# Attention on one Trainium2 core: the low parts of the probabilities on VectorE, made in halves of 256 columns

## The chip, the cores and the metric

One NeuronCore of a Trainium2 chip. The metric is the time of one launch of the whole program on the device, in microseconds (us). Engines are named as in the profile: PE is TensorE (PEld its weight loads), DVE is VectorE, ACT is ScalarE, POOL is GpSimd, SP is the queue that issues most DMAs.

## The reference

The input x has shape (2, 8, 256, 512): batch, channel, row, column. It is normalised by groups, goes through attention, and the result is added to x; then it is normalised again and goes through a sphere convolution, which is added too. Only the attention matters for this change:

```
q = _rope(split_heads(_conv(_mcl(x, Wq, bq), q_conv_w, q_conv_b, 3)))
k = _rope(split_heads(_conv(_mcl(x, Wk, bk), k_conv_w, k_conv_b, 3)))
v = split_heads(_conv(_mcl(x, Wv, bv), v_conv_w, v_conv_b, 3))
qk = jnp.einsum('bceqd,bcekd->bceqk', q, k) / math.sqrt(h)
a = jax.nn.softmax(qk, axis=-1)
o = jnp.einsum('bceqk,bcekd->bceqd', a, v)
return _conv(_mcl(o, Wo, bo), o_conv_w, o_conv_b, 0)
```

For each of the 2 x 8 pairs of batch entry and channel there are 8 heads with 512 queries, 512 keys and 32 features a head.

## The kernel before, in words

The program has three stages one behind the other, each with a block of its own: `front` (normalisation, projections, convolution, rotation), `attend` (attention), `blend` (mixing, second normalisation, sphere convolution). The change lies in `attend`, which in the profile runs from about 375 to about 890 us.

`attend` handles 16 units, one for each pair of batch entry and channel. A unit has 32 steps: 8 heads times 4 tiles of 128. Several things happen for each step, shifted against one another:

- **Row scores** (`row_scores`, L1197): PE multiplies 128 queries by all 512 keys into one of three PSUM banks called `a_row`. DVE takes the maximum of each row (`row_max`, L1265), and then the bank is free. The maxima of a unit are split in two (L1269), turned by PE (L1206, also into an `a_row` bank), copied by ACT (L1294) and put into the query tile as two more rows, so that the next pass subtracts them.
- **Column scores** (`col_scores`, L1217): PE makes the scores again, transposed, into one of three banks `a_col`; ACT takes the exponential into `a_prob`, float32 128x512 (L1306).
- **Low parts**: the matmuls that follow work in bfloat16. The upper 16 bits of each probability serve as its high part `ph`, read with a stride in the float32 tile. The low part is `prob` minus `ph`, written as bfloat16 into `a_pl`. Of the 32 steps of a unit, 26 are done by POOL (L1349) and six by DVE (L1276), those of `LOWS_ON_DVE = (1, 5, 9, 23, 26, 30)`. Both engines read two tensors from SBUF and write one. Below, such an instruction is called a low.
- **Sets**: after each four steps PE sums the weights (L1231) and mixes the values (L1240), 20 matmuls of 32 output rows each, four side by side. After four sets ACT makes the logarithm and the inverse of the weights (L1311, L1318) and DVE multiplies the mix by it (`divide`, L1284).
- **Tails**: PE multiplies the divided result by the output weights (L1254) into a further `a_row` bank, which is held for ten steps; ACT copies it out (L1324).

Each engine's instructions are written out in order by `pipeline(ops)`: every operation has a slot number, and an engine emits its operations slot by slot. Row work of step t of unit n has slot 32n + t; the low of that step has slot 32n + 43 + t on both engines, which is why lows of one unit lie between row maxima of the next two. The set g of a unit has slot 32n + 54 + 4g on PE, so 8 slots lie between the last low of a set and the set.

`row_places()` fixes at build time which of the three `a_row` banks a row score, a turn of the maxima or a tail gets: the one used longest ago that is not held. In the steady state the row score of place r in a unit (r = slot modulo 32) therefore waits for the row maximum of place r - 3 for r = 6 to 22. From r = 23 on to r = 4 of the next unit the tail, and after it the turn, takes one of the banks in the rotation, and the row score of place r waits for the row maximum of place r - 2. At r = 5 it waits for the bank of the turn, which the copy L1294 on ACT frees. I count places r in what follows: the lows of DVE stand behind the row maxima of places 2, 5, 9, 12, 16 and 20, the two divides behind those of places 3 and 19, the tail begins behind the set at place 22.

The waits of the row bank and of the set on PE:

```
s_row = bank_free(pe, ROW_PLACE[step])      # waits for max_done, among others
...
pe.wait_ge(lo_pool, pool_lows(n, g))
pe.wait_ge(lo_dve, dve_lows(n, g))
```

Of the kernel before, what the change touches and what calls it, by code (L numbers as in the profile page):

```python
# [20 lines left out]
ALU = mybir.AluOpType  # L21
# [3 lines left out]
B, C, F, W = 2, 8, 256, 512  # L25
# [908 lines left out]
def attend(nc, T, QK, V, Z, mixing, spaces, q0, k0, qk0_in, negmax0, ahead_in):  # L934
# [9 lines left out]
    with ExitStack() as ctx:  # L944
# [3 lines left out]
        STEPS = HEADS * QT  # L948
        UNITS = B * C
# [20 lines left out]
        prob = [sb(f"a_prob{s}", [P, QUAD, W]) for s in range(RING)]  # L970
        ph = [prob[s][:].bitcast(BF16).rearrange("p h (w t) -> p h w t", t=2)[:, :, :, 1] for s in range(RING)]
        pl = [sb(f"a_pl{s}", [P, QUAD, W], BF16) for s in range(RING)]
# [27 lines left out]
        lo_dve = sem("a_lo_dve")  # L1000
# [20 lines left out]
        def low_on_pool(t):  # L1021

            return t not in LOWS_ON_DVE

        def dve_lows(n, g):

            return len(LOWS_ON_DVE) * n + sum(t < QUAD * (g + 1) for t in LOWS_ON_DVE)

        def pool_lows(n, g):

            return STEPS * n + QUAD * (g + 1) - dve_lows(n, g)


        SPLIT = STEPS
        TURN = SPLIT + 3
        EXP = TURN + 7
        MIX = EXP + 3 * QUAD
        KEEP = MIX + QUAD * (QT - 1) + 1
        TAIL = KEEP + QUAD * QT + 3
        PARTS = 2  # L1040
        PART = W // PARTS
        assert TURN + STEPS < TAIL and TAIL + 2 * (QT + 1) < TURN + 2 * STEPS

        def pipeline(ops):

            at = [[] for _ in range(UNITS * STEPS + TAIL)]
            for t, f in ops:
                at[t].append(f)
            for slot in at:
                for f in slot:  # L1050
                    f()

        def steps(first, emit):
            return [(STEPS * n + first + t, lambda n=n, t=t: emit(n, t)) for n in range(UNITS) for t in range(STEPS)]

        def rows(emit):
            return [(STEPS * n + t, lambda n=n, t=t: emit(n, t)) for n in range(UNITS) for t in range(STEPS) if STEPS * n + t >= EARLY]

        def lows(first, emit, on_pool):
            return [(STEPS * n + first + t, lambda n=n, t=t: emit(n, t)) for n in range(UNITS) for t in range(STEPS) if low_on_pool(t) == on_pool]  # L1060

        def sets(first, emit):
            return [(STEPS * n + first + QUAD * g, lambda n=n, g=g: emit(n, g)) for n in range(UNITS) for g in range(SETS)]

        def quads(first, emit):
            return [(STEPS * n + first + QUAD * QT * m, lambda n=n, m=m: emit(n, m)) for n in range(UNITS) for m in range(SETS // QT)]

        def units(first, emit):
            return [(STEPS * n + first, lambda n=n: emit(n)) for n in range(UNITS)]

        def tails(first, emit):
            return [(STEPS * n + first + (QT + 1) * j, lambda n=n, j=j: emit(n, j)) for n in range(UNITS) for j in range(FH)]

        def tail_parts(first, emit):
            return [(STEPS * n + first + (QT + 1) * j + QT // PARTS * part, lambda n=n, j=j, part=part: emit(n, j, part))
                    for n in range(UNITS) for j in range(FH) for part in range(PARTS)]

        def row_places():
# [10 lines left out]

            for at in range(UNITS * STEPS + TAIL):  # L1090
                n, t = divmod(at - TURN, STEPS)
# [3 lines left out]
                if EARLY <= at < UNITS * STEPS:  # L1095
                    rows[at] = take(at)
                    maxima[rows[at][0]] = at + 1 - EARLY
                n, t = divmod(at - TAIL, STEPS)
                if t == 0 and 0 <= n < UNITS:
# [80 lines left out]
        def _(pe):  # L1180
# [39 lines left out]
            def mix_set(n, g):  # L1220
                kt, quad = g % QT, SETS // QT * n + g // QT
                p = (SETS * n + g) % RING
                pe.wait_ge(lo_pool, pool_lows(n, g))
                pe.wait_ge(lo_dve, dve_lows(n, g))
                if n == g == 0:
                    pe.wait_ge(ones_set, 1)
                if kt == 0 and quad:
                    pe.wait_ge(logged, quad)
                for part in (ph, pl):
                    for r in range(QUAD):  # L1230
                        nc.tensor.matmul(weight[r * DH:(r + 1) * DH, :], ones[:], part[p][:, r, :],  # L1231
                                         start=kt == 0 and part is ph, stop=kt == QT - 1 and part is pl)
                if g == 0:
                    pe.wait_ge(v_in[n % VALUES], 16 * (n // VALUES + 1))
                if kt == 0 and quad:
                    pe.wait_ge(divided, quad)
                for j, (vv, part) in enumerate(((vh, ph), (vl, ph), (vh, pl))):
                    for r in range(QUAD):
                        h = g // QT * QUAD + r
                        last = nc.tensor.matmul(mix[r * DH:(r + 1) * DH, :], vv[n % VALUES][:, kt, h * DH:(h + 1) * DH], part[p][:, r, :],  # L1240
                                                start=kt == j == 0, stop=kt == QT - 1 and j == 2)
                last.then_inc(mixed, 1)

            def tail(n, j, part):
# [8 lines left out]
                for f in range(FH):  # L1253
                    last = nc.tensor.matmul(out[n][:, at], wo[n % CHANNELS][:, f, j * P:(j + 1) * P], oT[n % 2][:, f, at], start=f == 0, stop=f == FH - 1)  # L1254
                if part == PARTS - 1:
                    last.then_inc(out_full, 1)

            pipeline(units(TURN, turn_max) + steps(EXP, col_scores) + rows(row_scores) + sets(MIX, mix_set) + tail_parts(TAIL, tail))

        @block.vector  # L1260
        def _(ve):
            def row_max(n, t):
                step = STEPS * n + t
                ve.wait_ge(row_full, step + 1 - EARLY)
                nc.vector.reduce_max(negmax[n % PAIR][:, 0, t:t + 1], row[ROW_PLACE[step][0]][:], AX.X, negate=True).then_inc(max_done, 1)  # L1265

            def split_max(n):
                ve.wait_ge(max_done, STEPS * (n + 1) - EARLY)
                nc.vector.tensor_tensor(negmax[n % PAIR][:, 1, :].rearrange("p (h t) -> p h t", t=QT), negmax[n % PAIR][:, 0, :].rearrange("p (h t) -> p h t", t=QT),  # L1269
                                        maxhigh[n % PAIR][:, 0:HEADS, :], ALU.subtract).then_inc(max_split, 1)  # L1270

            def low_part(n, t):
                step = STEPS * n + t
                p, r = step // QUAD % RING, t % QUAD
                ve.wait_ge(exp_done, step + 1)
                nc.vector.tensor_tensor(pl[p][:, r, :], prob[p][:, r, :], ph[p][:, r, :], ALU.subtract).then_inc(lo_dve, 1)  # L1276

            def divide(n, m):
                quad = SETS // QT * n + m
                if m == 0 and n >= 2:  # L1280
                    ve.wait_ge(out_full, FH * (n - 1))
                ve.wait_ge(mixed, QT * (quad + 1))
                ve.wait_ge(inverted, quad + 1)
                nc.vector.tensor_tensor(oT[n % 2][:, m, :], mix[:], inverse[quad % 2][:], ALU.mult).then_inc(divided, 1)  # L1284

            pipeline(rows(row_max) + units(SPLIT, split_max) + lows(EXP + 1, low_part, False) + quads(KEEP, divide))

        @block.scalar
        def _(act):
# [36 lines left out]
            def store_z(n, j):  # L1326
# [3 lines left out]
            pipeline(quads(KEEP, log_weight) + units(TURN + 1, keep_max) + units(TURN + 2, load_max) + steps(EXP, exp) + quads(KEEP, invert)  # L1330
                     + tails(TAIL + QT, keep_out) + tails(TAIL + QT + 1, store_z))
            for j in range(FH):
                act.wait_ge(z_stored[j], 16 * UNITS)

        @block.gpsimd
        def _(pool):
            nc.gpsimd.memset(ones[:], 1.0).then_inc(ones_set, 1)
            pool.wait_ge(ones_set, 1)
            nc.gpsimd.memset(wmix[:], 0.0).then_inc(wzero, 1)
            pool.wait_ge(wzero, 1)  # L1340
            nc.gpsimd.memset(w_taps[:, 1], 0.0).then_inc(wzero, 1)
            pool.wait_ge(const_in, 16)
            nc.gpsimd.tensor_copy(ident16[:], ident[:]).then_inc(ident16_set, 1)

            def low_part(n, t):
                step = STEPS * n + t
                p, r = step // QUAD % RING, t % QUAD
                pool.wait_ge(exp_done, step + 1)
                nc.gpsimd.tensor_tensor(pl[p][:, r, :], prob[p][:, r, :], ph[p][:, r, :], ALU.subtract).then_inc(lo_pool, 1)  # L1349

            pipeline(lows(EXP + 1, low_part, True))

# [559 lines left out]
```

## Time and profile before

| | |
|---|---|
| median of 3 runs | 1157.39 us (1154.14 to 1162.59) |
| the profiled execution, its own time | 1156.79 us |
| span of the profiled execution | 1154.9 us |
| PE busy | 1051.2 us (91%) |
| DVE busy | 827.7 us (72%) |
| ACT busy | 682.9 us (59%) |
| POOL busy | 745.9 us (65%) |

The span runs from the first to the last instruction of the profile; the time of the execution is 1.9 us longer. Busy times are averages over three stages with different limits. What a change inside `attend` is worth has to be read from the stretch between about 400 and 880 us, in which one unit follows another in the same pattern.

### The profile page before, as it was taken

The numbers are of one execution on the slowest core, as the hardware profiler recorded it, in microseconds if no ns is written. First come the engines' busy times: TensorE is split into PE (matmuls) and PEld (weight loads), VectorE is DVE, ScalarE is ACT, GpSimd is POOL, SyncE is SP. The second block draws the span as 40 slices with busy tenths as digits, with TensorE's granted clock in tenths as the row PEclk, the third lists the DMA queues.
The fourth block names the chain that finished last, engine by engine and source line by source line (L and its number), as shares of the span: only waits on it lengthen the run. The fifth ranks groups of instructions, "written<-read, shape, count | busy, mean of one in ns | idle before, by whom it ended". The sixth has DMA issues, their size and how long they took to land. (4 is left out here: it accounts for less than half of the span.)

```text
span 1154.9 us, 25535 instructions
## 1 busy us (share of the span) xinstructions
PE 1051.2 (91%) x10288; PEld 564.1 (49%) x10288; DVE 827.7 (72%) x1210; ACT 682.9 (59%) x1146; POOL 745.9 (65%) x768
## 2 busy tenths in 40 slices
PE   0899999999997999999999999999976888799997
PEld 0677777777773233333333333333323344354553
DVE  5888776666669988999888888888831865544343
ACT  3857677777652666666666666666664322446345
POOL 1144455545553799999999999899975129919900
PEclk9999999999997899999999999999988899999999
DMA  9934434341654939174544628191050999766661
GB/s 304 324 99 139 117 90 142 101 133 40 159 140 125 151 78 159 44 109 85 95 77 77 112 68 127 38 155 45 14 156 37 292 321 282 222 222 162 203 201 48
DMA packets 137589, 158.62 MB, mean 137 GB/s; under 512 B 17808, under 2 KB 85664, under 8 KB 137340
## 3 DMA queue, kind: packets, MB, share of 16 engines
q1 hardware_dynamic: 114368, 122.15, 44.0%
q10 hardware_dynamic: 14560, 25.66, 6.1%
q0 software_dynamic: 8544, 9.18, 3.1%
q8 instruction: 82, 1.34, 0.5%
q14 instruction: 35, 0.29, 0.1%
HBM read 106.11 MB, written 52.89 MB: 138 GB/s over the span
## 5 line engine op out<-in xcount | busy, mean ns | idle before, releaser
L1349 POOL TENSOR_TENSOR a_pl<-a_prob 128x512 bf16<-128x512 f32 x416 | 455.7, 1125 | 52.6 <-ACT a_prob L1306 50.8
L1306 ACT ACTIVATE a_prob<-a_col 128x512 f32<-128x512 f32 x512 | 279.7, 598 | 152.5 <-PE a_col L1217 151.9
L1265 DVE TENSOR_REDUCE a_negmax<-a_row 128x1 f32<-128x512 f32 x384 | 244.5, 679 | 40.8 <-PE a_row L1197 40.6
L548 PE MATMUL f_acc<-f_wh,f_xhl 128*32 128x384 bf16 x2560 | 163.5, 327 | 1.0 <-DVE f_yl L666 1.0
L666 DVE TENSOR_TENSOR f_yl<-f_acc,f_yh 128x768 bf16<-128x768 f32 x80 | 75.3, 956 | 75.8 <-ACT f_yh L780 75.8
L1276 DVE TENSOR_TENSOR a_pl<-a_prob 128x512 bf16<-128x512 f32 x96 | 108.4, 1130 | 24.8 <-ACT a_prob L1306 24.7
L903 POOL TENSOR_TENSOR f_straight<-f_straight,f_turned 128x832 f32<-128x832 f32 x40 | 85.5, 2137 | 59.4 <-DVE f_turned L692 59.4
L1622 PE MATMUL b_acc_s<-b_xh,b_mat_h 128*104 128x512 bf16 x256 | 99.5, 389 | 14.3 <-DVE b_xl L1706 13.2
L1197 PE MATMUL a_row<-a_k,a_q 96*128 96x512 bf16 x256 | 98.1, 383 | 10.9 <-DVE a_negmax L1265 8.9
L548 PE MATMUL f_acc<-f_wl,f_xhl 128*32 128x384 bf16 x1280 | 107.8, 326 | 0.0
L1217 PE MATMUL a_col<-a_q,a_k 98*128 98x512 bf16 x256 | 95.8, 387 | 7.6 <-DMA a_q<-a_maxrows 5.5
L1197 PE MATMUL a_row<-k,q 96*128 96x512 bf16 x228 | 90.9, 403 | 11.3 <-DVE a_negmax L1265 4.6
L1217 PE MATMUL a_col<-q,k 98*128 98x512 bf16 x256 | 99.2, 388 | 0.2 <-issue 0.2
L1624 PE MATMUL b_acc_s<-b_xh,b_mat_l 128*104 128x512 bf16 x256 | 98.3, 384 | 0.0
L1623 PE MATMUL b_acc_s<-b_xl,b_mat_h 128*104 128x512 bf16 x256 | 98.1, 383 | 0.0
L548 PEld LDWEIGHTS f_acc<-f_wh,f_xhl 128*32 128x32 bf16 x2560 | 68.9, 97 | 41.6 <-issue 7.4
L571 PE MATMUL f_acc_qk<-f_band_h,f_yh 128*128 128x208 bf16 x344 | 88.0, 256 | 0.9 <-ACT f_acc_qk L817 0.9
L572 PE MATMUL f_acc_qk<-f_band_l,f_yh 128*128 128x208 bf16 x344 | 87.6, 255 | 0.0
L573 PE MATMUL f_acc_qk<-f_band_h,f_yl 128*128 128x208 bf16 x344 | 87.5, 254 | 0.0
L1570 POOL DMA_DIRECT2D q<-XP x122 | 60.5, 505 | 34.1 <-ACT b_xn L1799 24.1
L1240 PE MATMUL a_mix<-a_prob,a_v 128*32 128x512 bf16 x1024 | 81.3, 392 | 1.2 <-DVE a_oT L1284 1.2
L1706 DVE TENSOR_TENSOR b_xl<-b_xn,b_xh 128x513 bf16<-128x513 f32 (+4 forms) x60 | 41.8, 697 | 50.5 <-ACT b_xh L1803 50.2
(166 smaller groups left out, 1989.6 us busy)
## 6 DMA issues: line engine op xcount, KB each, us to landing
X<-b_x ACTq DMA_DIRECT2D x16, 526.0 KB, 8.7
a_v<-V SPq DMA_DIRECT2D x16, 512.0 KB, 5.3
Z<-a_z ACTq DMA_DIRECT2D x32, 256.0 KB, 2.2
b_res<-X SPq DMA_DIRECT2D x38, 208.0 KB
out<-b_y ACTq DMA_DIRECT2D x38, 208.0 KB
V<-f_vout SPq DMA_DIRECT2D x64, 104.0 KB
b_raw<-X SPq DMA_DIRECT2D x24, 258.0 KB, 8.1
q<-in_x SPq DMA_DIRECT2D x6, 1024.0 KB, 6.5
```

Source lines behind the costliest of these rows:

```text
L548: last = nc.tensor.matmul(acc[half][c * KW:(c + 1) * KW, part, 0:PART], xx[g % 2][:, (half * QUAD + c) * FH + f, at], ww[half * QUAD + c][ ...
L571: nc.tensor.matmul(out, yh[half][s][:, feat], band_h[:, half, a, :], start=False, stop=False, skip_group_check=loose)
L572: nc.tensor.matmul(out, yh[half][s][:, feat], band_l[:, half, a, :], start=False, stop=False, skip_group_check=loose)
L1197: nc.tensor.matmul(row[s_row][:].rearrange("p (t w) -> p t w", t=QT), q[s][0:QK_ROWS, h, qt, m, :], k[s][0:QK_ROWS, h, :, m, :], start=Tru ...
L1217: nc.tensor.matmul(col[step % COLS][:].rearrange("p (t w) -> p t w", t=QT), k[s][:, h, kt, m, :], q[s][:, h, :, m, :], start=True, stop=Tr ...
L1265: nc.vector.reduce_max(negmax[n % PAIR][:, 0, t:t + 1], row[ROW_PLACE[step][0]][:], AX.X, negate=True).then_inc(max_done, 1)
L1276: nc.vector.tensor_tensor(pl[p][:, r, :], prob[p][:, r, :], ph[p][:, r, :], ALU.subtract).then_inc(lo_dve, 1)
L1306: nc.scalar.activation(prob[sets_done % RING][:, t % QUAD, :], col[step % COLS][:], ACT.Exp).then_inc(exp_done, 1)
L1349: nc.gpsimd.tensor_tensor(pl[p][:, r, :], prob[p][:, r, :], ph[p][:, r, :], ALU.subtract).then_inc(lo_pool, 1)
L1622: nc.tensor.matmul(to, mat_h[:, e, :], xh[s][:, at:at + W], start=first, stop=False)
L1623: nc.tensor.matmul(to, mat_h[:, e, :], xl[s][:, at:at + W], start=False, stop=False)
L1624: last = nc.tensor.matmul(to, mat_l[:, e, :], xh[s][:, at:at + W], start=False, stop=end)
```

## The change: what it does

On DVE, a low of 512 columns becomes two lows of 256 columns. The first half stays in its slot, the second half gets the slot behind it, so that one row maximum stands between the halves. Both wait for the same exponential. Six instructions of a unit become twelve, 96 of the kernel become 192. The set on PE waits for twice as many signals of DVE. POOL's lows stay whole. Nothing else is changed; `lows` is split into `pool_parts` and `low_halves`.

```
+        HALVES = 2
...
-        def lows(first, emit, on_pool):
-            return [(STEPS * n + first + t, lambda n=n, t=t: emit(n, t)) for n in range(UNITS) for t in range(STEPS) if low_on_pool(t) == on_pool]
+        def pool_parts(first, emit):
+            return [(STEPS * n + first + t, lambda n=n, t=t: emit(n, t)) for n in range(UNITS) for t in range(STEPS) if low_on_pool(t)]
+
+        def low_halves(first, emit):
+            return [(STEPS * n + first + t + half, lambda n=n, t=t, half=half: emit(n, t, half))
+                    for n in range(UNITS) for t in range(STEPS) if not low_on_pool(t) for half in range(HALVES)]
...
-                pe.wait_ge(lo_dve, dve_lows(n, g))
+                pe.wait_ge(lo_dve, HALVES * dve_lows(n, g))
...
-            def low_part(n, t):
+            def low_half(n, t, half):
                 step = STEPS * n + t
                 p, r = step // QUAD % RING, t % QUAD
+                at = slice(half * (W // HALVES), (half + 1) * (W // HALVES))
                 ve.wait_ge(exp_done, step + 1)
-                nc.vector.tensor_tensor(pl[p][:, r, :], prob[p][:, r, :], ph[p][:, r, :], ALU.subtract).then_inc(lo_dve, 1)
+                nc.vector.tensor_tensor(pl[p][:, r, at], prob[p][:, r, at], ph[p][:, r, at], ALU.subtract).then_inc(lo_dve, 1)
...
-            pipeline(rows(row_max) + units(SPLIT, split_max) + lows(EXP + 1, low_part, False) + quads(KEEP, divide))
+            pipeline(rows(row_max) + units(SPLIT, split_max) + low_halves(EXP + 1, low_half) + quads(KEEP, divide))
...
-            pipeline(lows(EXP + 1, low_part, True))
+            pipeline(pool_parts(EXP + 1, low_part))
```

The order changes on DVE alone. The first place is DVE's program around the first divide of a unit, from the split of the maxima (behind place 0) on; `a_negmax<-a_row` or `negmax<-a_row` is a row maximum, `a_pl<-a_prob` a low, `a_oT` the divide. Before:

```order
L1269 TENSOR_TENSOR a_negmax<-a_negmax 128x32
L1265 TENSOR_REDUCE negmax<-a_row 128x1 x2
L1276 TENSOR_TENSOR a_pl<-a_prob 128x512
L1265 TENSOR_REDUCE negmax<-a_row 128x1
L1284 TENSOR_TENSOR a_oT<-a_mix,a_inverse 128x512
L1265 TENSOR_REDUCE negmax<-a_row 128x1 x2
L1276 TENSOR_TENSOR a_pl<-a_prob 128x512
L1265 TENSOR_REDUCE negmax<-a_row 128x1 x4
```

And now:

```order
L1274 TENSOR_TENSOR a_negmax<-a_negmax 128x32
L1270 TENSOR_REDUCE negmax<-a_row 128x1 x2
L1282 TENSOR_TENSOR a_pl<-a_prob 128x256
L1270 TENSOR_REDUCE negmax<-a_row 128x1
L1282 TENSOR_TENSOR a_pl<-a_prob 128x256
L1290 TENSOR_TENSOR a_oT<-a_mix,a_inverse 128x512
L1270 TENSOR_REDUCE negmax<-a_row 128x1 x2
L1282 TENSOR_TENSOR a_pl<-a_prob 128x256
L1270 TENSOR_REDUCE negmax<-a_row 128x1
L1282 TENSOR_TENSOR a_pl<-a_prob 128x256
L1270 TENSOR_REDUCE negmax<-a_row 128x1 x3
```

The second half of the low of place 2 stands between the row maximum of place 3 and the divide; that of place 5 stands between the row maxima of places 6 and 7.

The second place is DVE's program around the second divide of the same unit, up to the row maxima that run beside the tails. Before:

```order
L1265 TENSOR_REDUCE negmax<-a_row 128x1 x4
L1276 TENSOR_TENSOR a_pl<-a_prob 128x512
L1265 TENSOR_REDUCE negmax<-a_row 128x1 x3
L1284 TENSOR_TENSOR a_oT<-a_mix,a_inverse 128x512
L1265 TENSOR_REDUCE negmax<-a_row 128x1
L1276 TENSOR_TENSOR a_pl<-a_prob 128x512
L1265 TENSOR_REDUCE negmax<-a_row 128x1 x11
```

And now:

```order
L1270 TENSOR_REDUCE negmax<-a_row 128x1 x3
L1282 TENSOR_TENSOR a_pl<-a_prob 128x256
L1270 TENSOR_REDUCE negmax<-a_row 128x1
L1282 TENSOR_TENSOR a_pl<-a_prob 128x256
L1270 TENSOR_REDUCE negmax<-a_row 128x1 x2
L1290 TENSOR_TENSOR a_oT<-a_mix,a_inverse 128x512
L1270 TENSOR_REDUCE negmax<-a_row 128x1
L1282 TENSOR_TENSOR a_pl<-a_prob 128x256
L1270 TENSOR_REDUCE negmax<-a_row 128x1
L1282 TENSOR_TENSOR a_pl<-a_prob 128x256
L1270 TENSOR_REDUCE negmax<-a_row 128x1 x10
```

The halves of the low of place 16 stand around the row maximum of place 17, those of place 20 around that of place 21; the row maximum of place 22, which frees the bank for the row score of place 24, has moved behind one more instruction.

## Rows read from the trace of the kernel before

**Rows 1.** Page, costliest groups: count | busy us, mean ns | idle before.
```profile
L1276 DVE TENSOR_TENSOR a_pl<-a_prob 128x512 bf16<-128x512 f32 x96 | 108.4, 1130 | 24.8 <-ACT a_prob L1306 24.7
```

**Rows 2.** Busy us of PE, PEld, DVE, ACT, POOL; then clock, DMA.
```profile
500.00:600.00 100.00, 95.66 (x776) 37.36 (x778) 89.10 (x133) 66.79 (x125) 91.39 (x84) 1.00 0.61 101
```

**Rows 3.** Waits of PE, 500 to 800 us: total us, times, longest.
```profile
PE a_row L1197 <- DVE a_negmax L1265: 8.5, 15, 0.8
PE a_row L1197 <- DVE negmax L1265: 2.3, 4, 0.8
```

**Rows 4.** One source line each: shortest, median, longest ns; first, last start.
```profile
L1276 DVE TENSOR_TENSOR a_pl<-a_prob x96: 693/1126/1558, 383.0 to 878.1; 128x512 bf16<-128x512 f32 x96
...
L1349 POOL TENSOR_TENSOR a_pl<-a_prob x250: 1033/1041/1490, 499.0 to 799.0; 128x512 bf16<-128x512 f32 x125
```

**Rows 5.** DVE in order of time: start us, length us, instruction, how many.
```profile
587.80 0.34 DVE L1269 TENSOR_TENSOR a_negmax<-a_negmax 128x32 f32<-128x32 f32 x1
588.06 1.27 DVE L1265 TENSOR_REDUCE negmax<-a_row 128x1 f32<-128x512 f32 x2
589.26 1.45 DVE L1276 TENSOR_TENSOR a_pl<-a_prob 128x512 bf16<-128x512 f32 x1
590.63 0.68 DVE L1265 TENSOR_REDUCE negmax<-a_row 128x1 f32<-128x512 f32 x1
591.37 0.69 DVE L1284 TENSOR_TENSOR a_oT<-a_mix,a_inverse 128x512 f32<-128x512 f32 x1
...
593.17 1.52 DVE L1276 TENSOR_TENSOR a_pl<-a_prob 128x512 bf16<-128x512 f32 x1
594.62 2.47 DVE L1265 TENSOR_REDUCE negmax<-a_row 128x1 f32<-128x512 f32 x4
597.01 1.12 DVE L1276 TENSOR_TENSOR a_pl<-a_prob 128x512 bf16<-128x512 f32 x1
...
599.86 0.82 DVE L1276 TENSOR_TENSOR a_pl<-a_prob 128x512 bf16<-128x512 f32 x1
...
602.99 1.13 DVE L1276 TENSOR_TENSOR a_pl<-a_prob 128x512 bf16<-128x512 f32 x1
...
607.10 0.84 DVE L1276 TENSOR_TENSOR a_pl<-a_prob 128x512 bf16<-128x512 f32 x1
607.87 2.54 DVE L1265 TENSOR_REDUCE negmax<-a_row 128x1 f32<-128x512 f32 x4
...
619.16 0.34 DVE L1269 TENSOR_TENSOR negmax<-negmax 128x32 f32<-128x32 f32 x1
```

**Rows 6.** POOL in order of time, 588 to 618 us, columns as before.
```profile
588.11 2.04 POOL L1349 TENSOR_TENSOR a_pl<-a_prob 128x512 bf16<-128x512 f32 x2
...
590.79 1.04 POOL L1349 TENSOR_TENSOR a_pl<-a_prob 128x512 bf16<-128x512 f32 x1 [0.64 <-ACT a_prob L1306]
...
593.11 2.48 POOL L1349 TENSOR_TENSOR a_pl<-a_prob 128x512 bf16<-128x512 f32 x2 [1.27 <-ACT a_prob L1306]
...
606.36 11.58 POOL L1349 TENSOR_TENSOR a_pl<-a_prob 128x512 bf16<-128x512 f32 x11 [0.34 <-ACT a_prob L1306]
```

**Rows 7.** PE in order of time: row scores and one mix.
```profile
591.80 0.38 PE L1197 MATMUL a_row<-k,q 96*128 96x512 bf16 x1 [0.85 <-DVE negmax L1265]
...
593.00 0.63 PE L1240 MATMUL a_mix<-a_prob,a_v 128*32 128x512 bf16 x8
...
595.35 0.39 PE L1197 MATMUL a_row<-k,q 96*128 96x512 bf16 x1 [0.32 <-DVE negmax L1265]
...
598.79 0.39 PE L1197 MATMUL a_row<-k,q 96*128 96x512 bf16 x1
...
605.97 0.39 PE L1197 MATMUL a_row<-k,q 96*128 96x512 bf16 x1
...
609.20 0.39 PE L1197 MATMUL a_row<-k,q 96*128 96x512 bf16 x1
```

**Rows 8.** ACT in order of time, the copy of the turned maxima.
```profile
591.13 0.57 ACT L1294 ACTIVATE a_maxrows<-a_row 16x512 bf16<-16x512 f32 x1
```

## The prediction

> **What bounds the kernel now.** I read the page first, for which stage is touched: the changed line L1276 is the low on DVE, 96 instructions with 1130 ns each [rows 1]. Then the stretch in which units follow one another: from 500 to 600 us PE is busy 95.66 us, DVE 89.10, POOL 91.39, ACT 66.79 [rows 2]. PE is the bound by a small margin, and two more engines have about a tenth to spare. Then what PE still waits for: 10.8 us of 300, all in front of row scores, put down to row maxima [rows 3]. So DVE is late in some places and idle in others, and the question is where. One unit takes 619.16 - 587.80 = 31.36 us (from split to split of the maxima, [rows 5]), and in order of time it shows two halves. From place 2 to place 22 DVE has no gap worth naming, and the row scores of places 9 and 13 (595.35 and 598.79) start some 0.05 us after the row maximum that frees their bank has ended. From the row score of place 24 on (609.20) PE sets the pace, with tails in between, and DVE waits for it. That score starts 0.05 us behind the end of the row maximum of place 22: the second of the four from 607.87 starts at 607.87 + 0.60 and takes 0.68, end 609.15 [rows 5, 7]. So the unit's length is a DVE chain from the first low (589.26) to the row maximum of place 22, and a PE chain behind it. What makes the DVE chain longer makes the unit longer, one for one.
>
> The wait of 0.85 us at 591.80 is named after a row maximum too, but by the order of banks it is the copy of the turned maxima on ACT, which ends at 591.70 [rows 7, 8]. The change leaves that one as it is.
>
> **What a low costs.** It takes 693 to 1558 ns on DVE and 1033 to 1490 on POOL, the same 128x512 each time [rows 4]. The order of time shows why. The low from 589.26 meets a POOL low that ends at 590.15, and ends at 590.71, 0.55 us (rounded) behind it. The one from 593.17 ends at 594.69, and POOL's next low, which had been started meanwhile, ends at 595.59, 0.90 behind it instead of 1.04 behind its own start [rows 5, 6]. So the two exclude one another: a DVE low waits to the end of the POOL low that runs, then needs 0.55; POOL's next then needs 0.90. POOL's own pace is (11.58 - 1.04 - 0.45)/10 = 1.01 us, 0.45 being the one long low among the eleven [rows 6]. The six lows of a unit last 1.45, 1.52, 1.12, 0.82, 1.13 and 0.84, in sum 6.88 us, of which 6 x 0.55 = 3.30 is work and 3.58 is waiting for POOL [rows 5].
>
> The Trainium skill states such a rule (SBUF — State Buffer, the section on SBUF's two separate sides): a DVE instruction with two SBUF inputs and a GpSimd instruction take a shared pair of ports for the whole instruction, and the loser blocks. The trace agrees, with the 0.55 and 0.90 above.
>
> **The change, part by part.** The order shows that it does what it says. A half has half the columns: behind a POOL low it should need 0.28 us (half of 0.55; were part of the 0.55 a fixed cost, more: from 0.34 us for 128x32 to 0.69 for a low alone [rows 4, 5] 256 columns make 0.19, which gives 0.55 - 0.19 = 0.36). I take 0.28, since the lock holds data movement, and keep 0.36 for the range. Each extra instruction starts 0.07 us before the one in front ends, as the rows do (2 x 0.60 + 0.68 for three maxima). Row maxima come every 0.60 us (2.47 for four).
>
> The walk through a unit, from the state at 589.26, with A and B for the halves:
> - Place 2: A asks at 589.26, POOL ends 590.15, A ends 590.44 (before: 590.71). The row maximum runs from 590.37, B asks at 590.97. POOL's low from 590.79 is running (it waited for its exponential) and ends 591.83; B ends 592.11. Divide from 592.04, before 591.37.
> - Place 5: two row maxima later A asks at 593.85; POOL's low from 593.11 ends 594.15; A ends 594.43 (before 594.69). B asks at 594.96. POOL's next, blocked by A, ends 594.43 + 0.90 = 595.33; B ends 595.61.
> - From here the pattern repeats: B always finds the POOL low that A held up, so it asks 0.53 behind A's end and waits 0.37. Place 9: A asks 597.34, waits 0.17, ends 597.79; B ends 598.97. Place 12: A asks 600.10, waits 0.37; B ends 601.93. Place 16: A asks 603.66, waits 0.17; B ends 605.29. Place 20: A asks 607.76 (divide in front, with ACT's inverse 0.65 later as the sets are), waits 0.31; the row maximum of place 21 starts 608.28, B ends 609.53.
> - The row maximum of place 22 runs 609.46 to 610.14, and the row score of place 24 can start at 610.20 instead of 609.20: 1.0 us more.
>
> As a sum: waits of A 0.90 + 0.30 + 0.17 + 0.37 + 0.17 + 0.31 = 2.22, of B 0.86 + 5 x 0.37 = 2.71, work 12 x 0.28 = 3.36; together 8.29 less 6 x 0.07 of overlap, against 6.88 before: +0.99 us. In between PE's row scores shift by -0.25 (place 9), +0.33 (10), +0.14 (13), +0.58 (21), inside the 1.0 and not on top of it. Behind place 24 PE sets the pace again, DVE waits for it as before, POOL's queue drains to the exponentials, and the next unit starts from the same state.
>
> What stays covered: the halves that signal the sets end up to 0.9 us later, but 8 slots, a quarter of a unit, lie between the last low and its set. The divide at place 3 ends at 592.73 instead of 592.06; the mix that waits for it starts at 593.00 [rows 7], so 0.2 us of cover is left. POOL gains: a full DVE low cost it 0.45, two halves 2 x (0.28 + 0.90 - 1.01) = 0.34. That is off the path in the units; behind the last row score the sets wait for POOL, and some six lows bring 6 x 0.1 = 0.5 us.
>
> Fifteen units have row scores beside lows. The first of them lacks the lows of places 2, 5 and 9, for which I take off 0.2. So 14.8 x 1.0 - 0.5 = +14.3 us. On the profiled execution (1156.79 us, 1.9 more than its span) that is 1171; the median lies 0.6 above it: **1171.5 us**, +1.2%.
>
> The Trainium skill has a rule that speaks against this change (VectorE: DVE Perf Modes, the sections on the TRN2 errata): a fixed cost for each instruction, with (N + 151)/0.96 ns for a float32 tensor-tensor of N columns, hence the advice to keep tiles at 512 or more. The low alone agrees (693 ns, the formula gives 691). By this page alone the split would cost 151/0.96 = 157 ns six times a unit, an estimate of +14 us in all; in my walk that start-up runs while DVE waits for POOL, and the second wait takes its place. No part of the sum uses this.
>
> **The rivals.**
> - *The growth is absorbed.* DVE is idle for 11% of the time [rows 2], 3.4 us a unit, and if the chain to place 22 had slack, 1.0 us would vanish: 1155 to 1162. Against it speaks that the row score of place 24 starts directly behind its row maximum, and that the idle time lies behind it.
> - *Faster: the smoothing wins.* The longest stop between row maxima falls from 1.52 to 1.2 us, and A's waits from 3.58 to 2.22, as the walk has it. If POOL did not get in between A and B, B would cost a half low alone, 0.69 - 0.27 = 0.42: 2.22 + 6 x 0.28 + 6 x 0.42 - 0.42 = 6.00, against 6.88, -0.9 us a unit, 1144. The change is a gain if B costs less than 0.57 on average; the walk has 0.73. Against it: POOL's next low is already started and blocked when DVE is done (it ends 0.90 later, not 1.04).
> - *Slower still: a half costs more.* With 0.36 in place of 0.28 twelve halves bring 0.96 more a unit, +29 in all, 1186. If A's waits stayed at 3.58, since the phase to POOL falls otherwise, it would be 2.35 a unit, 1192. It decides from a half's work of about 0.32.
>
> **How the numbers follow.** About 1% is what a measurement of this kernel tells from no change. My forecast gets 0.60, with 1165 to 1177 as its own range (an error of 0.4 us a unit); absorbed 0.17, faster 0.09, slower still 0.14. The range 1153 to 1183 holds the first two and about half of the paths towards the last. Over 1% slower begins at 1169: 0.72 of the forecast's chance and all of the last, 0.57. Within 1% are the rest of the forecast, the absorbed case and a little of the faster one, 0.36. Faster by over 1% is 0.07.
>
> **What would show it.** In the changed profile: 192 lows on DVE, most B halves near 0.65 us, and no A half over 1.3; a unit of 32.4 us from split to split; DVE busy near 92 of 100 us and PE near 93; PE's waits for row maxima about 1 us a unit more, at places 17 to 24; POOL's long lows near 1.2 us instead of 1.49. I am wrong if B halves come out near 0.43 (POOL does not get in), if units stay at 31.4 with longer DVE time (slack that I missed), or if the set at place 6 begins to wait for the divide.

## The result and the profile after

| | before | with halves |
|---|---|---|
| median of 20 runs | 1157.17 us (1153.19 to 1162.59) | 1164.94 us (1160.55 to 1169.30) |
| ratio | 1 | 1.0064, 95% interval 1.0048 to 1.0080 |
| span of the profiled execution | 1154.9 us | 1163.4 us |

The kernel with halves is slower by 7.8 us in the median, 8.5 in the profiled span. The forecast was 1171.5 us, +14.3 (range 1153 to 1183).

The stretch from 500 to 600 us, busy time of PE, PEld, DVE, ACT, POOL as in [rows 2]:

```profile
500.00:600.00 100.00, 92.99 (x755) 36.79 (x757) 88.88 (x147) 65.40 (x124) 84.96 (x80) 1.00 0.63 101
```

PE has lost 2.7 us of 100 and POOL 6.4, DVE is as busy as before. Everything runs slower beside a DVE that has more to do for each unit; POOL loses more than PE because its lows are also held up for less time (mean 1101 ns from 500 to 800 us, before 1128). PE's waits from 500 to 800 us, 10.8 us in [rows 3], are 16.2:

```profile
PE a_row L1202 <- DVE a_negmax L1270: 12.9, 23, 0.8
PE a_row L1202 <- DVE negmax L1270: 3.3, 6, 0.8
```

DVE in order of time, the same unit as in [rows 5]. The split of the maxima now stands at 594.55 instead of 587.80, so 6.75 us have to be taken off each time to compare:

```profile
594.55 0.34 DVE L1274 TENSOR_TENSOR a_negmax<-a_negmax 128x32 f32<-128x32 f32 x1
...
596.01 1.18 DVE L1282 TENSOR_TENSOR a_pl<-a_prob 128x256 bf16<-128x256 f32 x1
...
597.72 1.15 DVE L1282 TENSOR_TENSOR a_pl<-a_prob 128x256 bf16<-128x256 f32 x1
598.79 0.68 DVE L1290 TENSOR_TENSOR a_oT<-a_mix,a_inverse 128x512 f32<-128x512 f32 x1
...
600.58 0.59 DVE L1282 TENSOR_TENSOR a_pl<-a_prob 128x256 bf16<-128x256 f32 x1
...
601.70 0.66 DVE L1282 TENSOR_TENSOR a_pl<-a_prob 128x256 bf16<-128x256 f32 x1
...
604.08 0.46 DVE L1282 TENSOR_TENSOR a_pl<-a_prob 128x256 bf16<-128x256 f32 x1
...
615.58 0.66 DVE L1282 TENSOR_TENSOR a_pl<-a_prob 128x256 bf16<-128x256 f32 x1
616.16 1.87 DVE L1270 TENSOR_REDUCE negmax<-a_row 128x1 f32<-128x512 f32 x3
...
626.85 0.34 DVE L1274 TENSOR_TENSOR negmax<-negmax 128x32 f32<-128x32 f32 x1
```

The first halves shown take 1.18, 0.59 and 0.46 us, the second ones 1.15, 0.66 and 0.66. The twelve halves of the unit make 8.36 us, where the six lows made 6.88 [rows 5]. The row maximum of place 22 starts at 616.16, less 6.75 is 609.41. The unit takes 626.85 - 594.55 = 32.30 us, before 31.36. PE in the same unit, to be held against [rows 7]:

```profile
599.75 0.63 PE L1245 MATMUL a_mix<-a_prob,a_v 128*32 128x512 bf16 x8
...
603.01 0.39 PE L1202 MATMUL a_row<-k,q 96*128 96x512 bf16 x1 [0.57 <-DVE negmax L1270]
...
616.89 0.39 PE L1202 MATMUL a_row<-k,q 96*128 96x512 bf16 x1 [0.21 <-DVE negmax L1270]
```

The mix at place 6 starts at 599.75 less 6.75 = 593.00, as before. The row score of place 24 starts at 610.14 instead of 609.20.

The last split of the maxima, first of before, then with halves:

```profile
838.26 0.82 DVE L1269 TENSOR_TENSOR a_negmax<-a_negmax 128x32 f32<-128x32 f32 x1
```
```profile
852.49 0.82 DVE L1274 TENSOR_TENSOR a_negmax<-a_negmax 128x32 f32<-128x32 f32 x1
```

Up to here the profiled execution with halves is 14.23 us behind. Of these, 0.55 us is older than the change: the first split stands at 375.09 us before and at 375.64 with halves, and no low has run by then. From the first split to the last it is 13.68 us. At the end of the span 8.5 are left: 5.7 us came back in the last 310 us, in which no row maximum stands. The waits of PE behind this point show it, first before (836 to 870 us), then with halves (850 to 884):

```profile
PE a_col L1217 <- DMA a_q<-a_maxrows: 5.5, 1, 5.5
```
```profile
PE a_col L1222 <- DMA a_q<-a_maxrows: 0.3, 1, 0.3
```

The first column score of the last unit waits for the DMA that puts the turned maxima into the query tile. In order of time, the DMA issues of ACT and SP of before, in two answers:

```profile
838.52 0.33 ACTq L1328 DMA_DIRECT2D Z<-a_z  x1
...
841.94 0.67 ACTq L1298 DMA_DIRECT2D a_q<-a_maxrows  x1
```
```profile
840.61 0.37 SPq L241 DMA_DIRECT2D q<-Z  x1
```

And with halves:

```profile
852.75 0.33 ACTq L1334 DMA_DIRECT2D Z<-a_z  x1
...
856.17 0.67 ACTq L1304 DMA_DIRECT2D a_q<-a_maxrows  x1
```
```profile
857.04 0.37 SPq L241 DMA_DIRECT2D q<-Z  x1
```

SP waits for the store of Z shown here and then issues its loads for the next stage. Before, the first load came 2.1 us behind the issue of the store and 1.3 us ahead of the small copy of the maxima, which then had to share the DMA engines with the loads. With halves the first load came 4.3 us behind the store and so 0.9 us behind the copy, and the copy was quick.

The stall cost more than its 5.5 us. PE, which had been busy up to 844.2, stood still until 849.69, and for some us behind that the granted clock was at or near the lower of its two levels, 0.50 of full speed or 1.2 GHz. Busy times from 848 to 856 us of before, columns as in [rows 2]:

```profile
848.00:852.00 4.00, 2.31 (x21) 0.70 (x21) 0.00 (x0) 0.60 (x1) 0.95 (x1) 0.50 1.06 258
852.00:856.00 4.00, 4.00 (x32) 0.94 (x24) 0.69 (x1) 2.07 (x4) 1.82 (x3) 0.57 1.07 261
```

With halves the clock was 1.00 from 852 to 894 us. From the last split to the start of the last column score it took 38.7 us before and 31.4 with halves, so 7.3 us came back here: 5.2 of the wait and about 2 of the clock. Behind that score 1.6 us were lost again.

### The profile page after: what moved, and what is told of

It reads as the page before. It is cut to its first block and busy times, and to the rows that moved or that the text cites. A ratio compares the mean times of both kernels' runs of the same rounds, so it can differ in the third digit from the quotient of the medians.

```text
span 1163.4 us, 25631 instructions
## 1 busy us (share of the span) xinstructions
PE 1054.2 (91%) x10288; PEld 567.4 (49%) x10288; DVE 848.4 (73%) x1306; ACT 682.8 (59%) x1146; POOL 737.0 (63%) x768
## 5 line engine op out<-in xcount | busy, mean ns | idle before, releaser
L1355 POOL TENSOR_TENSOR a_pl<-a_prob 128x512 bf16<-128x512 f32 x416 | 447.4, 1104 | 68.6 <-ACT a_prob L1312 68.2
L1270 DVE TENSOR_REDUCE a_negmax<-a_row 128x1 f32<-128x512 f32 x384 | 248.4, 679 | 42.3 <-PE a_row L1202 42.2
L1282 DVE TENSOR_TENSOR a_pl<-a_prob 128x256 bf16<-128x256 f32 x192 | 137.6, 720 | 12.7 <-ACT a_prob L1312 12.5
L1628 PE MATMUL b_acc_s<-b_xh,b_mat_h 128*104 128x512 bf16 x256 | 100.3, 392 | 12.6 <-DVE b_xl L1712 11.5
```

Of the source, the lines that this page charges most:

```text
L1282: nc.vector.tensor_tensor(pl[p][:, r, at], prob[p][:, r, at], ph[p][:, r, at], ALU.subtract).then_inc(lo_dve, 1)
L1628: nc.tensor.matmul(to, mat_h[:, e, :], xh[s][:, at:at + W], start=first, stop=False)
```

## The experiments

All against runs of the kernel before on the same chip in the same job. "The gate" below is one more wait on SP: it issues its loads for the next stage only when the last copy of the turned maxima has landed.

**The loads held back, whole lows.** The kernel before and

```
+            sp.wait_ge(max_in[(UNITS - 1) % PAIR], 16 * ((UNITS - 1) // PAIR + 1))
             for g in range(AHEAD):
```

> The kernel before, but SP issues its loads for the next stage (Z and x, about 840 us) only after the last copy of the turned maxima has landed. My theory: in the trace of before, the last copy of the maxima was issued at 841.94, 1.3 us behind the first of those loads, and PE waited 5.5 us for it; in the changed kernel it was issued at 856.17, 0.9 us ahead of them, and PE waited 0.3 us. That is the part of the 14 us that the changed kernel does not show at its end. So here PE's wait falls from 5.5 to under 1 us, units stay at 31.36 us, and the time is 5 us (4 to 6) below before: ratio 0.9955. Rival, the missing part came in by chance or in the stage behind: the same time as before, within 1.5 us.

Measured: 1152.55 us against 1158.74, ratio 0.9958 (0.9939 to 0.9977). PE's wait for the copy:

```profile
PE a_col L1218 <- DMA a_q<-a_maxrows: 0.3, 1, 0.3
```

The gain of 6.2 us (the interval makes it 2.7 to 7.1) is the 5.2 us of the wait and something of the clock behind it, to within the measurement. In the profile the stretch behind the last split is 7.9 us shorter than before; 2.8 us were lost ahead of it, 2.0 of them in the second unit, from 400 to 437 us, where the granted clock was 0.95 and in the profile of before 1.00. Of the versions here that leave no low out this one has the lowest ratio; two more below, at 0.9970 and 0.9975, overlap with it.

**The same gate, with halves.** The same edit on the changed kernel.

> The changed kernel with the same gate on SP's loads. My theory: the copy of the maxima was ahead of the loads already, so nothing is won: within 1.5 us of the changed kernel in its profile, units at 32.3 us, and 13 to 15 us above the run with the gate alone, ratio to before about 1.0065 to 1.008. Rival (the split costs only 7.5 us wherever it is measured): 7 to 8 us above the run with the gate alone, about 1.002.

Measured: 1166.12 us, ratio 1.0064 (1.0042 to 1.0087); the changed kernel has the same ratio without the gate. Between the two gated kernels lie 13.6 us. So the split costs 13.6 us where the loads are out of the way, and nearly half of it (13.6 less 7.8) was made up by a collision that the kernel before had and the changed one had not.

**No row maximum between the halves.**

```
-            return [(STEPS * n + first + t + half, lambda ...
+            return [(STEPS * n + first + t, lambda ...
```

> The changed kernel, but both halves of a low stand directly behind one another, with no row maximum between. My theory (POOL's low that the first half held up gets the pair as soon as that half is done, and the second half has to wait for it to end, 0.90 us): the second half waits about 0.97 instead of 0.37 us, four times or more in a unit, a unit of 34.5 to 36.6 us, in all 1205 to 1235 us. Rival A (a split costs a fixed start-up for each instruction, whoever stands between): a unit of 32.3 us, 1165. Rival B (DVE keeps the pair from one half to the next): second halves of 0.3 to 0.4 us, a unit of 31.4 to 31.7 us, 1157 to 1162.

Measured: 1216.18 us, ratio 1.0517 (1.0475 to 1.0560). Two splits that lie two units apart, and the halves by source line:

```profile
618.34 0.34 DVE L1274 TENSOR_TENSOR a_negmax<-a_negmax 128x32 f32<-128x32 f32 x1
...
688.76 0.34 DVE L1274 TENSOR_TENSOR a_negmax<-a_negmax 128x32 f32<-128x32 f32 x1
```
```profile
L1282 DVE TENSOR_TENSOR a_pl<-a_prob x100: 407/1178/1297, 499.8 to 797.8; 128x256 bf16<-128x256 f32 x100
```
```profile
624.89 1.26 DVE L1282 TENSOR_TENSOR a_pl<-a_prob 128x256 bf16<-128x256 f32 x1
```

A unit takes 35.21 us here, (688.76 - 618.34)/2. A second half that follows at once lasts up to 1.26 us (the last line), of which 0.28 is work; where POOL has nothing to do a half takes 0.41. Rivals A (32.3) and B (31.4) are out: the same twelve instructions, 3 us a unit apart by their place alone, and DVE does not keep the pair of ports from one half to the next.

**Two row maxima between the halves.** `first + t + 2 * half`.

> The changed kernel, but two row maxima between the halves (the second half two slots behind the first). My theory (what the second half costs is its place in POOL's rhythm): it asks 1.13 us behind the end of the first, just after POOL has started the next low, and waits 0.78 instead of 0.37 us; walked through a unit as in the prediction this makes +3.0 us a unit, 34.4 us, in all 1190 to 1205 us. Rival A (fixed start-up for each instruction): a unit of 32.3 us, 1165. Rival C (more room between the halves spreads the load better): a unit below 32.3.

Measured: 1193.01 us, ratio 1.0309 (1.0272 to 1.0346). Again two units apart:

```profile
608.40 0.34 DVE L1274 TENSOR_TENSOR a_negmax<-a_negmax 128x32 f32<-128x32 f32 x1
...
676.80 0.34 DVE L1274 TENSOR_TENSOR a_negmax<-a_negmax 128x32 f32<-128x32 f32 x1
```
```profile
L1282 DVE TENSOR_TENSOR a_pl<-a_prob x106: 406/1054/1239, 507.3 to 799.4; 128x256 bf16<-128x256 f32 x106
```

34.20 us a unit, where the walk had 34.4. Neither more nor less room is better as such; by the walk one row maximum happens to let the second half ask when POOL has 0.37 us to go, two when it has 0.78, none when it has 0.97. These two runs have no gate, and PE waits 2.1 us (no row maximum) and 3.0 us (two) for the last copy in them; that is in their times and not in their units.

**Low parts from another place, whole.** The kernel with the gate and

```
-        LOWS_ON_DVE = (1, 5, 9, 23, 26, 30)
+        LOWS_ON_DVE = (13, 16, 19, 23, 26, 30)
```

> Whole lows and the gate on SP's loads, but DVE does the lows of steps 13, 16, 19, 23, 26 and 30 instead of 1, 5, 9, 23, 26 and 30: three lows move from places 12, 16 and 20, ahead of the row maximum that sets the unit, to places 24, 27 and 30, where DVE waits for PE. My theory (the row maxima up to place 22 are the chain): about 1 us of PE's waits for row maxima go, a unit of 30.3 to 30.9 us instead of 31.36, 1138 to 1147 us. Rival (POOL now has 14 lows one behind the other and its sets come late): PE waits for POOL at the sets, a unit of 31.4 or more, 1153 or above.

Measured: 1155.83 us, ratio 0.9975 (0.9958 to 0.9993). This missed: a unit of 31.49 us where I had expected 30.3 to 30.9, and a smaller gain than with the gate alone (0.9958). DVE and PE from place 27 on show why, where before DVE stood idle:

```profile
617.52 0.69 DVE L1266 TENSOR_REDUCE negmax<-a_row 128x1 f32<-128x512 f32 x1 [0.30 <-PE a_row L1198]
618.12 1.43 DVE L1277 TENSOR_TENSOR a_pl<-a_prob 128x512 bf16<-128x512 f32 x1
619.48 1.27 DVE L1266 TENSOR_REDUCE negmax<-a_row 128x1 f32<-128x512 f32 x2
```
```profile
618.84 0.38 PE L1198 MATMUL a_row<-k,q 96*128 96x512 bf16 x1
...
620.22 0.39 PE L1198 MATMUL a_row<-k,q 96*128 96x512 bf16 x1
...
623.32 0.39 PE L1198 MATMUL a_row<-k,q 96*128 96x512 bf16 x1 [0.28 <-DVE negmax L1266]
```

From place 23 on only two banks go round, since the tail holds the third. A low of 1.43 us keeps the next row maximum until 619.48 to 620.16, and the row score two places on starts 0.06 us behind that, at 620.22. Behind the next low it is the same, and there PE stands idle for 0.28 us: the row maximum ends at 623.26, the row score starts at 623.32. DVE's idle time there is no slack: each row score needs its maximum within one place. The rival's numbers came true here (31.4 or more, 1153 or above), but its cause did not: PE waits for POOL at no set from 500 to 800 us, and its weight loads wait for POOL for 5.9 us, where it is 14.3 with the gate alone. That the gain in time is smaller than the gate's lies within the two intervals, and part of it is another thing: the second unit took 35.8 us at a granted clock of 0.91, with the gate alone 33.6 at 0.95.

**The same places, in halves.**

> The same places with every low of DVE in two halves a slot apart, as in the changed kernel. My theory (halves cost only ahead of place 22, where DVE is the chain; behind it they vanish in DVE's idle time): the cost of the split falls from 0.94 us a unit to 0 to 0.4, so 0 to 6 us above the run with whole lows at these places. Rival (a split costs about 0.16 us of DVE for each low wherever it stands, or PE is hurt in some other way): again 0.9 us a unit, 13 to 14 us above.

Measured: 1169.74 us, ratio 1.0098 (1.0070 to 1.0126). PE's waits from 500 to 800 us, first with whole lows at these places, then with halves:

```profile
PE a_row L1198 <- DVE a_negmax L1266: 11.4, 23, 0.8
PE a_row L1198 <- DVE negmax L1266: 2.9, 6, 0.8
```
```profile
PE a_row L1203 <- DVE a_negmax L1271: 19.4, 23, 1.1
PE a_row L1203 <- DVE negmax L1271: 5.0, 6, 1.1
```

32.56 us a unit, 1.07 above whole lows at the same places, 13.9 us in all. The rival of this run holds: the split costs about 1 us a unit wherever the lows stand. My part of the theory that it costs only ahead of place 22 falls.

**Two lows moved.** `LOWS_ON_DVE = (1, 13, 17, 23, 26, 30)`, whole, with the gate.

> Whole lows, the gate, and steps 1, 13, 17, 23, 26 and 30 on DVE: two lows moved instead of three, so that POOL has at most 9 and 11 lows in a row. By my theory the low that stays at place 12 keeps part of the chain: a unit of 30.5 to 31.1 us, 1140 to 1150, a little above the run with three moved. If POOL's row of 14 lows is what limits that one, this one is faster than it.

Measured: 1155.14 us, ratio 0.9970 (0.9952 to 0.9987), 31.31 us a unit. The same miss, and it cannot be told from three moved. PE's waits for row maxima are 11.6 us of 300, with the gate alone 11.7, so none were won; that the reason is the same as with three moved is argued from this.

**One SBUF input, in halves.** With the gate; `a_scratch` has a column for each half, and POOL first clears `a_pl`. The low parts of the six steps are left out.

```
-                nc.vector.tensor_tensor(pl[p][:, r, at], prob[p][:, r, at], ph[p][:, r, at], ALU.subtract).then_inc(lo_dve, 1)
+                nc.vector.reduce_max(scratch[:, 2 * step + half:2 * step + half + 1], prob[p][:, r, at], AX.X).then_inc(lo_dve, 1)
```

> The changed kernel with the gate, but the halves on DVE are replaced by maxima over the same 256 columns of the probabilities: one SBUF input instead of two, the same places, waits and signals. The low parts of these six steps are left out (zero or of an earlier step). My theory (what a half costs beside its work is the wait for POOL, and that comes from two engines that both read two tensors from SBUF): each half takes 0.35 to 0.45 us at most and always the same, POOL's lows never take 1.2 or 1.49 but 1.04 throughout, DVE stops to be the chain up to place 22, and the unit falls from 32.31 to 30.2 to 30.8 us, 1136 to 1147. Rival (the split costs start-up and DVE's time, whatever POOL does): the unit stays above 31.5.

Measured: 1134.02 us, ratio 0.9800 (0.9775 to 0.9825), 30.23 us a unit. The replaced halves and POOL's lows, by source line:

```profile
L1284 DVE TENSOR_REDUCE a_scratch<-a_prob x119: 402/409/413, 499.8 to 787.9; 128x1 f32<-128x256 f32 x119
```
```profile
L1359 POOL TENSOR_TENSOR a_pl<-a_prob x259: 1035/1039/1043, 499.7 to 799.2; 128x512 bf16<-128x512 f32 x130
```

No half waits, and no low of POOL is held up, although both engines still read the same tiles. DVE is no longer the chain either. All that PE waits for row maxima from 500 to 800 us is once a unit, for the turned maxima:

```profile
PE a_row L1204 <- DVE a_negmax L1272: 6.8, 8, 0.8
PE a_row L1204 <- DVE negmax L1272: 1.7, 2, 0.8
```

The edit changes more than the inputs: a maximum writes one column and not 256. That the output is not what makes DVE wait is shown by the divide of the kernel before, which has one input in SBUF and one in PSUM and writes 512 columns of float32 to SBUF: all 32 take 675 to 693 ns, also where POOL is in the middle of a low, as at 591.37 us [rows 5, 6].

**One SBUF input, whole.** The same with one maximum over 512 columns.

> The same with whole maxima over 512 columns in place of the six lows, with the gate (low parts of these steps left out as in the run with halves). My theory: without POOL in the way a split costs DVE only 6 times 0.1 us a unit and nothing is left of the 0.94 us: within 0.3 us a unit of the run with halves, within 4 us in all. Rival (fixed start-up of about 0.16 us for each instruction on the chain): 0.9 us a unit and 13 us below it.

Measured: 1136.92 us, ratio 0.9816 (0.9791 to 0.9842), 30.22 us a unit. The whole maximum takes 675 ns, two halves 818. Less 70 ns of overlap that is 0.07 us a low and 0.4 a unit of DVE's time, and nothing of it reaches the unit. The intervals of the two runs overlap. Without POOL in the way the split costs nothing that can be measured. But DVE has stopped to be the chain in both, so a fixed cost of 0.07 us a low would not show in the unit either; against that rival this pair proves less than the two runs with other gaps. The units are what to compare here: the second unit took 36.1 us in both, at a granted clock of 0.91, which is in their times.

**POOL's lows in halves.** The kernel with the gate, DVE's lows whole; `lo_pool` counts twice.

```
+                for half in range(2):
+                    at = slice(half * (W // 2), (half + 1) * (W // 2))
```

> The kernel before with the gate, DVE's lows whole, but each of POOL's 26 lows of a unit in two halves of 256 columns, one directly behind the other. My theory (a DVE low waits for the POOL instruction that runs, so shorter ones make it wait less): DVE's lows last 0.7 to 1.1 us instead of 0.82 to 1.52, their sum falls from 6.9 to about 5.3 us a unit. If POOL needs at most 1.1 us for two halves the unit falls to 30.5 to 31.2 and the time to 1141 to 1151; if POOL's own start-up makes it 1.25 or more, POOL becomes the bound (26 x 1.25 = 32.5) and the kernel is slower than before, 1165 to 1200. I take the second for the likelier, 6 to 4.

Measured: 1223.93 us, ratio 1.0581 (1.0552 to 1.0611), 35.8 us a unit: the second of the two cases, but further out than its range. By source line:

```profile
L1352 POOL TENSOR_TENSOR a_pl<-a_prob x832: 602/608/1109, 381.4 to 953.3; 128x256 bf16<-128x256 f32 x167
```
```profile
L1277 DVE TENSOR_TENSOR a_pl<-a_prob x96: 675/933/11529, 383.5 to 951.6; 128x512 bf16<-128x512 f32 x96
```

A half costs POOL 608 ns and a whole low 1041 [rows 4]. DVE's lows do become shorter (933 in the middle instead of 1126), and the theory of this run holds so far: PE's waits for row maxima from 500 to 800 us fall from 10.8 us to 0.8. POOL is not the bound either, as the second case had it: two halves make 1.22 us, 26 of them 31.6, and PE waits for POOL at no set. What PE waits for is the split of the maxima, which it has to turn:

```profile
PE a_row L1207 <- DVE a_negmax L1270: 18.0, 6, 3.0
PE a_row L1207 <- DVE negmax L1270: 6.0, 2, 3.0
```

That is 3.0 us in each unit, and none before. The last section shows the instruction behind it. Each such wait is followed by a stretch at the lower clock; behind the one that ends at 622.88 us:

```profile
626.00:630.00 4.00, 4.00 (x25) 0.50 0.02 6
```

(Busy time of PE alone, then clock and DMA.) From 500 to 800 us the granted clock was 0.91 of full speed, where it was 1.00 before. An estimate from the busy times of these 300 us: PE's idle time in a unit grows from 1.3 to 3.2 us, its busy time for the same work from 30.1 to 32.7. So of the 4.5 us that a unit is longer, about 1.9 are waiting and 2.6 the clock. No run parts the two.

## Why the prediction was right, and where it was off

**The bound and the lock were right.** The pair of ports that DVE and POOL exclude each other from was read from four durations, and what the runs with other gaps and with one input show fits it. Halves on DVE end 0.28 us behind the POOL low in front of them, POOL's longest low fell from 1490 to 1225 ns (the walk: about 1.2), and with one SBUF input on DVE both effects are gone. The Trainium skill's rule (SBUF — State Buffer, SBUF: two separate sides) agrees with this.

**The walk was right to 0.1 us.** It had the first halves of places 2, 5 and 9 at 1.18, 0.58 and 0.45, the second at 1.14, 0.65 and 0.65; the trace has 1.18, 0.59, 0.46 and 1.15, 0.66, 0.65, and the other six agree as well. It had the row score of place 24 at 610.20, the trace has 610.14. It had a unit 1.0 us longer, the trace 0.94. The divide's thin cover of 0.2 us held. One of its signs did not come: DVE busy near 92 of 100 us, measured 88.88. The prediction's own sum gives 89 (27.9 us of a unit before, 1.0 more, in 32.4), so 92 was a slip and says nothing on the mechanism.

**The 0.36 for a half's work came from a wrong reading.** It took 0.34 us as the time of a 128x32 instruction alone. The split at 587.80 [rows 5] is not alone: it ends at 588.14, and the POOL low in front of it at 588.09. Where POOL had not begun, at 375.09, the same instruction took 0.18. From 0.18 to 0.69 us, 256 columns make 0.27, and 0.55 less 0.27 is the 0.28 that was measured.

**The step that was mis-sized is the last one**, "14.8 x 1.0 - 0.5 = +14.3". For the 14.8 x 1.0 the trace has 13.68 us from the first split to the last. Behind it I had only POOL's 0.5 us, where the trace has 5.7 us coming back. What I left out is that the kernel before had a stall of 5.5 us of its own there, a single wait of PE for one small DMA behind SP's loads, with a stretch at the lower clock behind it, and that a shift of these loads against ACT by 2.2 us takes both away. The two gated kernels measure it: 6.2 us off the one, nothing off the other, 13.6 between them. The stall was to be seen in the profile of before, in the waits of PE behind 836 us; I had read PE's waits only from 500 to 800 us, and took the end of the stage to be shifted as it was. That the stall would go could not have been worked out from there; that its fate was open could, and the range should have said so.

**Where it was luck.** The measured 1164.94 us lies in the range of 1153 to 1183, but just outside the 1165 to 1177 that the forecast gave itself, and 6.6 us below 1171.5. The change is +0.64%: "over 1% slower" had 0.57, and what came true, "within 1%", had 0.36. Nearly half of that 0.36 was the absorbed case, and it did not happen: the units are 0.94 us longer. That 14.23 at the last split looks like the +14.3 is chance too, since 0.55 of it stood there before the first low.

**A step that came out right for a reason that was too narrow.** I held that DVE is the chain up to place 22 and idle behind it, so that what is late there is absorbed. The runs with lows at places 24, 27 and 30 say otherwise: the split costs 1.07 us a unit there too, since with two banks each row maximum must follow within a place. The prediction did not need that, because the changed kernel has no low behind place 22. The rival "absorbed" was weaker still than I thought.

**The fixed cost of an instruction is not the cause.** The Trainium skill (VectorE: DVE Perf Modes, the TRN2 errata) would have the split cost 157 ns of start-up six times a unit, an estimate of +14 us, near the 13.6 measured. The runs part the two: with the same twelve instructions a unit lasts 35.21, 32.30 or 34.20 us by the gap between halves. The fixed cost is there and is hidden. With POOL out of the way 32, 256 and 512 columns with two SBUF inputs take 0.18, 0.41 and 0.69 us. Behind a POOL low they end 0.05, 0.28 and 0.55 us after it, which goes with the number of columns and is 0.13 or 0.14 us less each time. Two halves behind two POOL lows need 0.56 us of work between them, one whole low 0.55; what they pay for is the second wait.

**What stays open.** Why SP could issue its loads 2.1 us behind the store of Z before and 4.3 us behind it with halves. The trace of the changed kernel has a DMA of the instruction queue among the store's packets:

```profile
q10 hardware_dynamic: 144, 0.26, 16.6%
q8 instruction: 1, 0.02, 1.4%
```

(DMA queues from 852.7 to 857 us: packets, MB, share.) The other traces fit. In the five that have such a packet between the store's issue and its landing (with halves, with halves and gate, both other gaps, POOL in halves) the store landed after 4.2, 3.9, 3.2, 3.5 and 3.5 us. Of the seven that have none, six show the landing, 2.0 us in each. That an instruction fetch in that place holds the store up is argued from this and was not tried. Nor is the order of copy and loads all there is to the stall: with two row maxima between the halves the copy was issued 0.2 us ahead of the first load, and PE still waited 3.0 us. That the medians of 20 runs lie 7.8 us apart and not 13.6 says that it is no accident of one execution.

## What to carry to other kernels

When two engines exclude each other from a pair of ports, the cost of an instruction there is its own work plus what is left of the other's, and cutting it in two buys a second such wait; whether that pays is read from where in the other engine's rhythm each piece asks, not from the size of the pieces. Idle time of an engine is slack only if nothing has to come back from it within that time: count the buffers that go round at that place. And before a sum is carried to the end of the program, look for single long waits behind the changed stretch, since a shift can remove or make one. Such a wait of PE can cost more than its length: 7.3 us came back for one that was 5.2 us shorter, because the granted clock was down behind it.

## What was unexpected of the hardware

With POOL's lows in halves the split of the maxima, a DVE instruction of 128x32 that takes 0.34 us in the kernel before and 0.18 without POOL, lasted 4.70. It was so in 15 of the 16 units (4.66 us or more), and PE waited 49.7 us for these 15 in all; the run is 66 us slower than the kernel before. In order of time, DVE and then POOL:

```profile
618.12 4.70 DVE L1270 TENSOR_TENSOR a_negmax<-a_negmax 128x32 f32<-128x32 f32 x1
```
```profile
617.60 5.17 POOL L1352 TENSOR_TENSOR a_pl<-a_prob 128x256 bf16<-128x256 f32 x9
```

Nine short POOL instructions went through, one behind the other, and DVE ended only when POOL had run out of work at 622.77. With whole POOL lows DVE always came next behind the one that ran: all its 96 lows ended within 1.56 us [rows 4]. So the turn that a waiting DVE instruction gets between long POOL instructions is not assured between short ones. It is not always lost either: in the row of 44 POOL halves from 631.87 us, none of DVE's four lows took more than 0.98 us. One low on DVE even took 11.5 us. What decides it was not tried.
